# Another order of the Sync engine's transfers, and one small GpSimd sum moved, in a fused attention and feed-forward kernel

## The chip, the cores and the metric

The kernel runs on one core of one Trainium2 chip. The metric is the device time of one execution in microseconds (us). A core has five engines with an instruction stream each: TensorE (PE in the profile, with PEld for its weight loads), VectorE (DVE), ScalarE (ACT), GpSimd (POOL) and the Sync engine (SP), which computes nothing and here issues most of the DMA transfers. Engines meet only at semaphores.

## The reference, cut to what matters

There are 8 batches of 512 rows with 512 columns. `x` attends to the context `ctx` of its own batch, with a mask on the probabilities, and a quantised feed-forward layer follows; both add to `x`.

```python
n = _layernorm(x)                                   # rows of x, eps 1e-5
scores = einsum('bqd,bkd->bqk', n, ctx) / 0.72
attn = softmax(scores) * mask
o = einsum('bqk,bkd->bqd', attn, ctx) + attn_bias
x = x + einsum('bqd,de->bqe', o, weights)
n = _layernorm(x)
s = max(amax(abs(n), axis=-1), 1e-6) / 127.0
q = clip(round(n / s), -128, 127)                   # int8, one scale per row
x = x + (q @ weight_q.T) * s * weight_scale + ffn_bias
```

## The kernel before, in words

The 4096 rows are 32 tiles of 128 rows, four to a batch. A tile goes through the engines in one step each of several stages, so that in step `d` scores are made of tile `d`, its probabilities are used for attention a step or two later, the integers of tile `d-4` go through the feed-forward product, and the normalised rows of tile `d+1` and the context tile `d+4` are made ready. Products in float32 are made of three float32r products of a high and a low part (`product3`, lines 636 to 638), so each operand is split: ACT copies the high part (`ct_hi`, `xt_hi`, `pt_hi`, `vw_hi`), DVE or POOL subtracts it for the low part (`ct_lo`, `xt_lo`, `pt_lo`, `vw_lo`).

Every engine runs `step(base, d)` over the same tiles, written out by hand (`run_steps`): four steps of the head (tiles 0 to 3), three rounds of eight steps that form the loop (tiles 4 to 27), and the tail (tiles 28 to 31 and what is left). The order within a step is the order of the code; there is no scheduler.

Three operands have to be transposed. In the loop this is done by 32x32 blocks: a DMA brings blocks to the right place, 4 transfers of 64 KB, and a DVE transpose turns inside each block. The normalised rows take the way `x_norm` -> `norm_rows` in HBM (issued by ACT) -> `x_blocks` (SP, `load_rows`) -> DVE `xt_raw`. The probabilities take the way `probs` -> `prob_rows` in HBM (SP, `store_probs`) -> `p_blocks`, which is the memory of `wq_rows` in the rows of the profile (SP, `load_probs`) -> DVE `pt_raw` -> ACT `pt_hi` -> DVE `pt_lo` -> PE `ps_attn`. The context goes straight from its input to `ctx_in`, two tiles by 4 transfers of 128 KB, and DVE turns each tile into `ct_raw`. The integers `x1_int` (`x_int` in the profile) are turned by a DMA transpose (`turn_integers`).

So SP's step is a fixed list: on even `d` the context pair `d+4, d+5`; the integers of tile `d-4`, for which it waits for ACT line 970; the rows of `d+1`; the store of the probabilities of `d-1`; `x` of tile `d+4`; the mask of `d+2`; and the load of the probabilities of `d-1`, for which it waits until their store has landed (line 535). SP works one transfer at a time, so whatever stands behind a waiting one is late too. SP's step `d` runs while the other engines are in the later part of their step `d-1`: the probabilities it stores have just been made.

ACT's step ends with two DMA issues, and before the second it waits for POOL's `out_tile` (`add_up`, line 1526). POOL gets to `out_tile` only after `inverse_deviation` (lines 1569 and 1572, the 1/sqrt of the second layernorm), which waits for ACT's sum of squares (line 1017). ACT's next step begins with `ct_hi` (line 878), rounding (958) and the integers (970), and line 896 sums up the `x` tile `d+4` that SP has loaded.

In the tail the last tile (`LAST`, 31) goes in halves. Its scale on DVE (`gains`, line 1269) needs its rstd from POOL (line 1572).

Of the kernel before, what the change touches and what calls it, by code (L numbers as in the profile page):

```python
# [37 lines left out]
P = 128  # L38
# [3 lines left out]
BLOCK = 32  # L42
QUADS = P // BLOCK
# [53 lines left out]
def exists(base, n):  # L97

    return 0 <= base + n < TILES
# [17 lines left out]
def slot(n, ring):  # L117

    return (PHASE + n) % ring
# [68 lines left out]
def xattn_ffn_kernel(nc, x, ctx_rows, mask, weights, attn_bias, weight_q, weight_scale, ffn_bias, out):  # L188
# [8 lines left out]
    with ExitStack() as stack:  # L197
# [239 lines left out]
        def is_tile(base, n, tile):  # L437

            return isinstance(base, int) and base + n == tile
# [28 lines left out]
        def _(sp):  # L468
# [3 lines left out]
            def load_blocks(into, src, row, n, tiles, loaded):  # L472
# [4 lines left out]
                for b in range(QUADS):  # L477
                    blocks = into[b * BLOCK:(b + 1) * BLOCK, k:k + tiles, :]
                    sp.dma_start(blocks.rearrange("i t (a c) -> i (t a) c", a=QUADS),  # L479
                                 rows[:, :, b * P:(b + 1) * P]).then_inc(loaded[k // 2], 16)  # L480

            def load_rows(base, n, row):

                quads = norm_rows[bass.ds(row, P), :].rearrange("(a i) d -> i a d", i=BLOCK)
                wait_rows(sp, norm_rows_stored, base, n)
                for b in range(QUADS):
                    blocks = x_blocks[b * BLOCK:(b + 1) * BLOCK, slot(n, 4), :]
                    sp.dma_start(blocks.rearrange("i (a c) -> i a c", a=QUADS),  # L488
                                 quads[:, :, b * P:(b + 1) * P]).then_inc(x_blocks_loaded[slot(n, 2)], 16)
# [61 lines left out]
            def step(base, d, row):  # L551

                bounced = in_loop(base)
                n = d + 4
                if n % 2 == 0 and exists(base, n) and not is_tile(base, n, PER_BATCH) \
                        and not is_tile(base, n, PER_BATCH + 2):

                    wait_count(sp, ct_raw_ready, base, n - 4 + 2 - PER_BATCH)
                    load_blocks(ctx_in, ctx_flat, row + n * P, n, 2, ctx_loaded)
                n = d - 4  # L560
                if exists(base, n) and (in_loop(base) or base + n < BY_PE):
                    turn_integers(base, n)
                n = d + 1
                if is_tile(base, n, BY_PE_ROWS):

                    sp.wait_ge(w_lo_ready, NT)
                    sp.wait_ge(bias_terms_ready, NT)
                if exists(base, n) and not is_tile(base, n, 1) and (not last_batch(base) or d == 0):
                    load_rows(base, n, row + n * P)
                if bounced:  # L570
                    store_probs(base, d - 1, row + (d - 1) * P)
                n = d + 4
                if exists(base, n):

                    wait_count(sp, x1_ready, base, n - 8 + 1)
                    load_x(row + n * P, slot(n, 8))
                n = d + 2
                if exists(base, n):

                    wait_count(sp, probs_ready, base, n - 4 + 1)  # L580
                    load_mask(row + n * P, slot(n, 4))
                if is_tile(base, d, 1):
                    load_ffn_constants()
                    sp.wait_ge(wq_rows_ready, 1)
                    for o in range(NT):
                        sp.dma_start_transpose(wq_t[:, :, o * P:(o + 1) * P], wq_rows[:, o, :]) \
                            .then_inc(wq_turned, 16)
                if is_tile(base, d, PER_BATCH - 1):

                    sp.wait_ge(wq_turned, 16 * NT)  # L590
                if bounced:
                    load_probs(base, d - 1, row + (d - 1) * P)
                n = d - 5
                if is_tile(base, n + 1, LAST):
                    store_out(base, n, row + n * P)
                    for h in range(2):

                        sp.wait_ge(last_out_ready, h + 1)
                        sp.dma_start(out_rows[LAST * P:TILES * P, half_of(h)], last_out[:, half_of(h)]) \
                            .then_inc(last_stored, 16)  # L600
                elif last_batch(base) and d > 0:
                    store_out(base, n, row + n * P)
                if last_batch(base) and d < 2:
                    load_rows(base, d + 2, row + (d + 2) * P)
# [863 lines left out]
        def _(pool):  # L1468
# [51 lines left out]
            def step(base, d):  # L1520
# [109 lines left out]
                if last_batch(base) and exists(base, d - 1):  # L1630
                    if is_tile(base, d - 1, TAIL):
                        inverse_deviation(d - 2)
                    if not is_tile(base, d - 1, LAST):
                        inverse_deviation(d - 1)
                    if is_tile(base, d - 1, TAIL):
                        add_up(d - 4)
                        add_ffn_bias(d - 2)
                    else:
                        add_ffn_bias(d - 2)
                        add_up(d - 4)  # L1640
                    if is_tile(base, d - 1, LAST):
                        inverse_deviation(d - 1)
                    if is_tile(base, d - 1, LAST):
                        add_ffn_bias(d - 1)
                if is_tile(base, d - 2, LAST):
# [33 lines left out]
```

## Time and profile before

| | us |
|---|---|
| median of 3 runs | 329.21 (328.72 to 329.78) |
| the profiled execution, its time | 328.42 |
| the profiled execution, its span | 326.6 |
| PE busy | 311.9 (95%) |
| DVE busy | 261.0 (80%) |
| POOL busy | 259.3 (79%) |
| ACT busy | 240.6 (74%) |

The span runs from the first to the last instruction; 1.8 us of the execution lie around it. An engine's idle time matters only where somebody waits for that engine. In the timeline, a row is start, duration, engine, line, operation and tiles, and in brackets how long the engine sat idle before it and what ended that. "xN" after a row merges N of a kind. SPq and ACTq are the issue of DMAs by SP and ACT; a transfer lands later than its issue ends.

### The profile page before, as it was taken

Reading aid. Unit: us, or ns where it says so; the run is one execution under the profiler, and the core shown is the slowest. Engines: PE = TensorE matmul, PEld = TensorE weight load, DVE = VectorE, ACT = ScalarE, POOL = GpSimd, SP = SyncE. Lnnn points to the kernel's source line nnn. Section 1 sums busy time; section 2 is a strip of 40 time slices with the busy share of each in tenths; the row PEclk is TensorE's granted clock in tenths of the full one; section 3 lists DMA queues with packets and bytes.
Section 4 is the critical chain, followed back from the end, with each engine's and each line's share of the span. In section 5 each row is a group of like instructions: output and inputs, shape, how many; then the busy total and the mean of one; then the engine's idle time right before and its main releaser. Section 6 shows DMA issues by size and latency. Waiting matters only on the chain.

```text
span 326.6 us, 5339 instructions
## 1 busy us (share of the span) xinstructions
PE 311.9 (95%) x1418; PEld 239.5 (73%) x1418; DVE 261.0 (80%) x565; ACT 240.6 (74%) x494; POOL 259.3 (79%) x362
## 2 busy tenths in 40 slices
PE   8999989999999999899998999999999999999982
PEld 7888767777777678677776777767778676776671
DVE  2998765988886899688887888788888778879775
ACT  5467867887887788788876889788787878866440
POOL 3274587897999789799997989899898879858683
PEclk9999999999999999999999999999999999999999
DMA  7995985798968979997888969998897996451112
GB/s 215 264 228 186 200 216 192 220 219 249 247 202 261 238 228 194 271 229 232 259 243 228 265 200 238 243 251 237 244 243 201 234 241 192 147 159 49 50 63 98
DMA packets 88173, 68.39 MB, mean 209 GB/s; under 512 B 25040, under 2 KB 67792, under 8 KB 88144
## 3 DMA queue, kind: packets, MB, share of 16 engines
q1 hardware_dynamic: 80368, 53.90, 65.3%
q10 hardware_dynamic: 7776, 14.16, 12.0%
q8 instruction: 11, 0.18, 0.3%
q14 instruction: 18, 0.15, 0.2%
HBM read 41.16 MB, written 22.54 MB: 195 GB/s over the span
## 4 chain that ended last, share of the span: by engine, by line
SPq 24%; DMA 22%; POOL 15%; ACT 11%; issue 9%; PE 9%; DVE 7%; ACTq 1%; POOLq 0%; DVEq 0%
DMA prob_rows<-probs 10%; DMA wq_rows<-prob_rows 8%; SPq L488 8%; SPq L535 7%; POOL out_tile L1526 5%; SPq L543 5%; SPq L479 4%; ACT x_round L958 2%; ACT ps_ct L1017 2%; POOL rstd L1572 2%; DVE pt_raw L1223 2%; ACT ct_hi L878 2%; ACT x_int L970 2%; POOL x_in L1560 2%; DMA norm_rows<-x_norm 1%
## 5 line engine op out<-in xcount | busy, mean ns | idle before, releaser
L636 PE MATMUL ps_attn<-vw_hi,pt_hi 128*128 128x512 f32 x120 | 47.9, 399 | 3.6 <-DVE pt_lo L1123 3.6
L636 PE MATMUL ps_scores<-ct_hi,xt_hi 128*128 128x512 f32 x124 | 48.7, 393 | 1.1 <-POOL xt_lo L1541 1.0
L638 PE MATMUL ps_scores<-ct_hi,xt_lo 128*128 128x512 f32 x124 | 48.3, 389 | 0.0
L637 PE MATMUL ps_scores<-ct_lo,xt_hi 128*128 128x512 f32 x124 | 48.3, 389 | 0.0
L638 PE MATMUL ps_attn<-vw_hi,pt_lo 128*128 128x512 f32 x120 | 46.8, 390 | 0.0
L637 PE MATMUL ps_attn<-vw_lo,pt_hi 128*128 128x512 f32 x120 | 46.8, 390 | 0.0
L1248 DVE TENSOR_TENSOR probs<-ps_scores,mask_in 128x512 f32<-128x512 f32 x32 | 22.0, 687 | 26.7 <-ACT ps_scores L981 26.3
L878 ACT ACTIVATE ct_hi<-ct_raw 128x512 fp32r<-128x512 f32 x28 | 17.7, 632 | 33.1 <-POOL out_tile L1526 30.4
L1560 POOL TENSOR_TENSOR x_in<-x_in,bias_w 128x512 f32<-128x512 f32 x32 | 41.5, 1296 | 0.7 <-issue 0.7
L1541 POOL TENSOR_TENSOR xt_lo<-xt_raw,xt_hi 128x512 fp32r<-128x512 f32 x29 | 37.7, 1301 | 4.1 <-ACT xt_hi L913 4.1
L1526 POOL TENSOR_TENSOR out_tile<-ffn_out,x_plus 128x512 f32<-128x512 f32 x28 | 39.6, 1415 | 0.0
L1586 POOL TENSOR_TENSOR x_plus<-x,ffn_bias_wide 128x512 f32<-128x512 f32 x28 | 36.3, 1297 | 3.7
L1533 POOL TENSOR_TENSOR ct_lo<-ct_raw,ct_hi 128x512 fp32r<-128x512 f32 x28 | 36.7, 1309 | 2.8 <-ACT ct_hi L878 2.8
L1139 DVE STREAM_TRANSPOSE xt_raw<-x_blocks 128x512 f32<-128x512 f32 x30 | 33.1, 1103 | 1.1 <-DMA x_blocks<-norm_rows 1.1
L810 PE MATMUL ps_ffn<-wq_t,xq_t 128*128 128x512 bf16 x120 | 31.1, 382 | 0.8 <-ACT xq_t L952 0.7
L1139 DVE STREAM_TRANSPOSE ct_raw<-ctx_in 128x512 f32<-128x512 f32 x28 | 30.8, 1099 | 0.0
L636 PEld LDWEIGHTS ps_attn<-vw_hi,pt_hi 128*128 128x128 f32 x120 | 22.5, 188 | 11.0 <-DVE pt_lo L1123 6.5
L888 ACT ACTIVATE x_norm<-x_in,norm 128x512 f32<-128x512 f32 x32 | 25.7, 804 | 5.2 <-POOL norm L1508 5.2
L636 PEld LDWEIGHTS ps_scores<-ct_hi,xt_hi 128*128 128x128 f32 x124 | 23.3, 188 | 7.1 <-POOL xt_lo L1541 2.4
L958 ACT ACTIVATE x_round<-x_neg,round_magic,neg_gain 128x512 f32<-128x512 f32 x31 | 24.9, 803 | 3.7 <-DVE neg_gain L1277 3.7
L636 PE MATMUL ps_vw<-w_hi,ct_hi 128*128 128x512 f32 x64 | 27.3, 427 | 0.0
L638 PEld LDWEIGHTS ps_scores<-ct_hi,xt_lo 128*128 128x128 f32 x124 | 23.3, 188 | 4.9
(187 smaller groups left out, 820.8 us busy)
## 6 DMA issues: line engine op xcount, KB each, us to landing
x_in<-in_x_dram SPq DMA_DIRECT2D x32, 256.0 KB, 4.1
mask_in<-in_mask_BxSxS_fk_dram SPq DMA_DIRECT2D x32, 256.0 KB, 4.4
norm_rows<-x_norm ACTq DMA_DIRECT2D x30, 256.0 KB, 4.0
x_blocks<-norm_rows SPq DMA_DIRECT2D x120, 64.0 KB, 2.4
ctx_in<-in_ctx_dram SPq DMA_DIRECT2D x56, 128.0 KB, 3.9
prob_rows<-probs SPq DMA_DIRECT2D x24, 256.0 KB, 2.3
wq_rows<-prob_rows SPq DMA_DIRECT2D x96, 64.0 KB, 3.5
out_dram<-out_tile ACTq DMA_DIRECT2D x24, 256.0 KB, 4.3
```

Of the source, the lines that this page charges most:

```text
L488: sp.dma_start(blocks.rearrange("i (a c) -> i a c", a=QUADS), quads[:, :, b * P:(b + 1) * P]).then_inc(x_blocks_loaded[slot(n, 2)], 16)
L636: nc.tensor.matmul(bank_, lhs_hi(t), rhs_hi(t), start=(t == 0), stop=False)
L637: nc.tensor.matmul(bank_, lhs_hi(t), rhs_lo(t), start=False, stop=False)
L638: last = nc.tensor.matmul(bank_, lhs_lo(t), rhs_hi(t), start=False, stop=(t == NT - 1))
L810: last = nc.tensor.matmul(ffn_bank(base, n)[:, :], xq_t[:, slot(n, 2), t, :], wq_t[:, t, :], start=(t == 0), stop=(t == NT - 1))
L958: nc.scalar.activation(x1_round[:, slot(n, 2), :], x1_neg[:, slot(n, 2), :], ACT.Identity, bias=round_magic[:, 0:1], scale=col(neg_gain, n ...
L1139: nc.vector.transpose(into.rearrange("p t (a i) -> p t a i", a=QUADS), blocks.rearrange("p (a j t) -> p t a j", a=QUADS, t=NT)).then_inc(r ...
L1526: nc.gpsimd.tensor_tensor(out_tile[:, slot(n, 2), :], ffn_out[:, slot(n, 2), :], x1_plus_of(base, n), ALU.add).then_inc(out_ready, 1)
L1533: nc.gpsimd.tensor_tensor(ct_lo[:, batch_of(n), :, j * P:(j + 1) * P], ct_raw[:, slot(n, 2), :, :], ct_hi[:, batch_of(n), :, j * P:(j + 1) ...
L1541: nc.gpsimd.tensor_tensor(flat(xt_lo[:, slot(n, 2), :, :]), flat(xt_raw[:, slot(n, 2), :, :]), flat(xt_hi[:, slot(n, 2), :, :].bitcast(F32 ...
L1560: nc.gpsimd.tensor_tensor(x_in[:, slot(d, 8), :], x_in[:, slot(d, 8), :], bias_w[:, :], ALU.add).then_inc(x_plus_ready, 1)
L1586: nc.gpsimd.tensor_tensor(into, x1_of(base, n), ffn_bias_wide[:, :], ALU.add).then_inc(x1_plus_ready, 1)
```

## The change

SP's step is put in another order, in all steps of the loop. The store of the probabilities comes right behind the integers, ahead of the rows. Their load comes right behind the rows, ahead of `x` and the mask. The context pair is loaded at the end of the step, and its four transfers are parted: two at the end of an even step, two at the end of the odd one after it, and the pair that a step asks for is one further on (`n = d + 6 - d % 2`), so its first half is issued at the end of step `n-6` instead of all of it at the start of step `n-4`. The number of transfers, their sizes and their bytes stay.

The second part is on POOL in the tail: in the step behind the last tile's scores, `inverse_deviation` of the last tile stands ahead of the two sums `add_ffn_bias(d - 2)` and `add_up(d - 4)` instead of behind them.

```diff
+            def load_half_pair(base, n, h):
+                wait_count(sp, ct_raw_ready, base, n - 4 + 2 - PER_BATCH)
+                k = slot(n, 4)
+                rows = ctx_flat[bass.ds((base + n) * P, 2 * P), :].rearrange("(a i) d -> i a d", i=BLOCK)
+                for b in range(h * QUADS // 2, (h + 1) * QUADS // 2):
+                    blocks = ctx_in[b * BLOCK:(b + 1) * BLOCK, k:k + 2, :]
+                    sp.dma_start(blocks.rearrange("i t (a c) -> i (t a) c", a=QUADS),
+                                 rows[:, :, b * P:(b + 1) * P]).then_inc(ctx_loaded[k // 2], 16)
...
                 bounced = in_loop(base)
-                n = d + 4
-                if n % 2 == 0 and exists(base, n) and not is_tile(base, n, PER_BATCH) \
-                        and not is_tile(base, n, PER_BATCH + 2):
-
-                    wait_count(sp, ct_raw_ready, base, n - 4 + 2 - PER_BATCH)
-                    load_blocks(ctx_in, ctx_flat, row + n * P, n, 2, ctx_loaded)
                 n = d - 4
                 if exists(base, n) and (in_loop(base) or base + n < BY_PE):
                     turn_integers(base, n)
+                if bounced:
+                    store_probs(base, d - 1, row + (d - 1) * P)
                 n = d + 1
...
                     load_rows(base, n, row + n * P)
                 if bounced:
-                    store_probs(base, d - 1, row + (d - 1) * P)
+                    load_probs(base, d - 1, row + (d - 1) * P)
                 n = d + 4
...
-                if bounced:
-                    load_probs(base, d - 1, row + (d - 1) * P)
+
+                n = d + 6 - d % 2
+                if exists(base, n) and base + n >= 2 * PER_BATCH:
+                    load_half_pair(base, n, d % 2)
...
                     else:
+                        if is_tile(base, d - 1, LAST):
+                            inverse_deviation(d - 1)
                         add_ffn_bias(d - 2)
                         add_up(d - 4)
-                    if is_tile(base, d - 1, LAST):
-                        inverse_deviation(d - 1)
```

This is SP in the middle of the loop before: an even step with the context, then an odd one without. The line number is followed by the tile written and the tile read; `x4` are four transfers.

```order
L479 DMA ctx_in<-in_ctx_dram 32x8x128 x4
L543 DMA_TRANSPOSE xq_t<-x_int 128x4x128
L488 DMA x_blocks<-norm_rows 32x4x128 x4
L526 DMA prob_rows<-probs 128x512
L470 DMA x_in<-in_x_dram 128x512
L492 DMA mask_in<-in_mask_BxSxS_fk_dram 128x512
L535 DMA wq_rows<-prob_rows 32x4x128 x4
L543 DMA_TRANSPOSE xq_t<-x_int 128x4x128
```

The same engine in the same place now, one step and the first transfer of the next.

```order
L554 DMA_TRANSPOSE xq_t<-x_int 128x4x128
L537 DMA prob_rows<-probs 128x512
L499 DMA x_blocks<-norm_rows 32x4x128 x4
L546 DMA wq_rows<-prob_rows 32x4x128 x4
L470 DMA x_in<-in_x_dram 128x512
L503 DMA mask_in<-in_mask_BxSxS_fk_dram 128x512
L490 DMA ctx_in<-in_ctx_dram 32x8x128 x2
L554 DMA_TRANSPOSE xq_t<-x_int 128x4x128
```

The four context transfers of every second step have become two in every step, at its end. The store has moved ahead of four row transfers, and the load has moved ahead of `x` and the mask, so `x` now has four more transfers ahead of it.

The last instructions of POOL before; `out_tile` is the sum that is stored, `rstd` the 1/sqrt.

```order
L1526 TENSOR_TENSOR out_tile<-ffn_out,x_plus 128x512
L1586 TENSOR_TENSOR ctx_in<-x,ffn_bias_wide 128x512
L1526 TENSOR_TENSOR out_tile<-ffn_out,ctx_in 128x512
L1569 TENSOR_TENSOR var_eps<-meanvar,eps 128x1
L1572 TENSOR_TENSOR rstd<-var_eps,minus_half 128x1
L1586 TENSOR_TENSOR ct_raw<-ctx_in,ffn_bias_wide 128x512
L1526 TENSOR_TENSOR out_tile<-ffn_out,ctx_in 128x512 x2
```

And now:

```order
L1535 TENSOR_TENSOR out_tile<-ffn_out,x_plus 128x512
L1578 TENSOR_TENSOR var_eps<-meanvar,eps 128x1
L1581 TENSOR_TENSOR rstd<-var_eps,minus_half 128x1
L1595 TENSOR_TENSOR ctx_in<-x,ffn_bias_wide 128x512
L1535 TENSOR_TENSOR out_tile<-ffn_out,ctx_in 128x512
L1595 TENSOR_TENSOR ct_raw<-ctx_in,ffn_bias_wide 128x512
L1535 TENSOR_TENSOR out_tile<-ffn_out,ctx_in 128x512 x2
```

The two 1-column instructions have moved ahead of two 512-column ones.

## Rows read from the trace of the kernel before

**Rows 1.** Waits in the loop, 56 to 275 us: total, times, longest

```profile
PEld ps_attn L636 <- DVE pt_lo L1123: 6.5, 8, 1.4
...
DVE pt_raw L1223 <- DMA wq_rows<-prob_rows: 10.5, 11, 1.7
...
ACT ps_xt L896 <- DMA x_in<-in_x_dram: 1.1, 2, 0.6
```

**Rows 2.** Timeline of PE, the feed-forward product of three steps

```profile
57.33 1.04 PE L810 MATMUL ps_ffn<-wq_t,xq_t 128*128 128x512 bf16 x4
...
102.73 1.04 PE L810 MATMUL ps_ffn<-wq_t,xq_t 128*128 128x512 bf16 x4
...
273.35 0.82 PE L810 MATMUL ps_ffn<-wq_t,xq_t 128*128 128x512 bf16 x3
```

**Rows 3.** Windows, whole loop: busy by engine, PEclk, DMA share, GB/s

```profile
57.33:273.35 216.02, 212.40 (x921) 161.24 (x921) 179.41 (x391) 172.99 (x366) 188.56 (x253) 1.00 0.88 236
```

**Rows 4.** Timeline of SP, an odd step and the start of the even one

```profile
226.25 1.21 SPq L543 DMA_TRANSPOSE xq_t<-x_int  x1
227.50 1.99 SPq L488 DMA_DIRECT2D x_blocks<-norm_rows  x4
229.54 0.43 SPq L526 DMA_DIRECT2D prob_rows<-probs  x1
...
231.84 1.76 SPq L535 DMA_DIRECT2D wq_rows<-prob_rows  x4
233.65 2.65 SPq L479 DMA_DIRECT2D ctx_in<-in_ctx_dram  x4
236.40 1.19 SPq L543 DMA_TRANSPOSE xq_t<-x_int  x1
```

**Rows 5.** Timeline of ACT, then of DVE, in the same step

```profile
225.53 0.63 ACT L970 ACTIVATE x_int<-x_round 128x512 bf16<-128x512 f32 x1
...
227.26 0.59 ACT L896 ACTIVATE ps_xt<-x_in 128x512 f32<-128x512 f32 x1
...
235.00 0.63 ACT L970 ACTIVATE x_int<-x_round 128x512 bf16<-128x512 f32 x1
...
226.87 0.69 DVE L1248 TENSOR_TENSOR probs<-ps_scores,mask_in 128x512 f32<-128x512 f32 x1 [1.10 <-ACT ps_scores L981]
...
234.12 1.10 DVE L1139 STREAM_TRANSPOSE xt_raw<-x_blocks 128x512 f32<-128x512 f32 x1
...
237.86 0.70 DVE L1223 STREAM_TRANSPOSE pt_raw<-wq_rows 128x512 f32<-128x512 f32 x1
```

**Rows 6.** Timeline of ACT, the integers in two undisturbed steps

```profile
84.05 0.63 ACT L970 ACTIVATE x_int<-x_round 128x512 bf16<-128x512 f32 x1
...
92.99 0.63 ACT L970 ACTIVATE x_int<-x_round 128x512 bf16<-128x512 f32 x1
```

**Rows 7.** DMA issues of the page: count, KB each, us to landing

```profile
x_blocks<-norm_rows SPq DMA_DIRECT2D x120, 64.0 KB, 2.4
...
prob_rows<-probs SPq DMA_DIRECT2D x24, 256.0 KB, 2.3
wq_rows<-prob_rows SPq DMA_DIRECT2D x96, 64.0 KB, 3.5
```

**Rows 8.** Landings of the x_in transfers, 50 to 275 us

```profile
DMA to landing us min/median/max: 2.9/4.1/5.0
```

**Rows 9.** Timeline of POOL, DVE and SP at the end of the tail

```profile
317.15 0.55 POOL L1572 TENSOR_TENSOR rstd<-var_eps,minus_half 128x1 f32<-128x1 f32 x1
...
320.73 2.60 POOL L1526 TENSOR_TENSOR out_tile<-ffn_out,ctx_in 128x512 f32<-128x512 f32 x2 [1.81 <-DVE ffn_out L1202]
...
314.42 0.21 DVE L1304 BATCH_NORM_AGGREGATE meanvar<-last_stats 128x2 f32<-128x12 f32 x1
...
317.81 0.21 DVE L1269 TENSOR_SCALAR q_range<-abs_max,rstd 128x1 f32<-128x1 f32 x1 [1.70 <-POOL rstd L1572]
...
323.73 0.93 SPq L599 DMA_DIRECT2D out_dram<-ct_raw  x2
```

## The prediction, written before the changed kernel was run

> **What bounds the kernel now.** I read the waits of the loop first. PE's weight loads stop eight times for the low part of the probabilities, 6.5 us in all, and DVE stops eleven times, 10.5 us in all, for the transfer that brings the probabilities back from HBM [rows 1]. The reader is to see one name at both: the way of the probabilities is what comes late, and PE waits at its end. PE's own timeline gives the size. From 57.33 to 102.73 there are five steps, 9.08 us each; from 102.73 to 273.35 there are 18 in 170.62 us, 9.48 each [rows 2]. PE is busy for 212.40 of the 216.02 us [rows 3]. So 9.08 is PE's floor for a step, and the loop's 23 steps stand 216.02 - 23 x 9.08 = 7.2 us above it. That is all that an order of transfers can win there.
>
> Is there a second floor close by? ACT, POOL and DVE go round in a ring: sum of squares, rstd, `out_tile`, `ct_hi`, integers. In a stretch without waits for DMA the integers start at 84.05 and 92.99, 8.94 apart [rows 6]. That is only 0.14 below PE's 9.08, so what delays ACT by more than 0.14 in every step is seen in the time.
>
> Then SP's timeline says why the probabilities are late. Call S the start of the integers' transpose, 226.25; ACT made them at 226.16 (225.53 + 0.63), so SP is punctual [rows 4, 5]. It issues the rows until 229.49, the store until 229.97, `x` and the mask, waits for the store, loads the probabilities at 231.84 and, as the next step is even, the context at 233.65 for 2.65. It is through at 236.30, and the next transpose starts at 236.40, though its integers were there at 235.63: 0.8 late [rows 4, 5]. The last of the four loads is issued some 1.3 into its 1.76, at 233.2, and lands 3.5 later [rows 7], at 236.7; DVE wants it at 237.86 [rows 5]. A punctual step has 1.2 to spare, and one that starts 0.8 late, with some extra in a landing, has nothing.
>
> **The change in the loop, step by step from S.** The transpose is out at S + 1.25 (227.50). The store needs `probs`, ready at 226.87 + 0.69 = 227.56, S + 1.31 [rows 5]; SP notices some 0.1 later (226.16 against 226.25), so the store goes at S + 1.4. That is a new wait of 0.15, and everything in SP's step stands behind it. Rows: S + 1.87 to 3.86 (0.43 for the store, 1.99 for the four). The store lands 2.3 after its issue [rows 7], at S + 3.7, so the wait for it has gone behind the rows. Load: S + 3.9 to 5.66. `x`: at S + 5.7 for 0.43, and the mask about as long, to S + 6.6. Half the context: 2.65 / 2 = 1.3, to S + 8.0. The next integers come at S + 9.08, so SP has 1.1 to spare in every step, where before the pair of steps had no reserve in its even half.
>
> Who gets what, and when:
> The probabilities: last load at S + 5.2, landed at 8.7 with the same 3.5, wanted at 237.86 = S + 11.6. Spare 2.9 instead of 1.2. The waits of [rows 1] should go, and with them their echo on ACT, POOL and PE.
> The rows: last of four at S + 3.4, + 2.4 = S + 5.8, wanted at 234.12 = S + 7.9. Spare 2.1 instead of 2.7; no cost.
> The context: the second half is out at the end of a step and is wanted about a step and a half later; no cost, and the wait in front of it is for turns two steps old.
> `x` of tile d+4: this is the loser. It was issued at S + 3.8, right behind the store, and now goes at S + 5.7. ACT wants it at 227.26 + 9.08 = S + 10.1 [rows 5]. With the median landing of 4.1 it is there at S + 9.8, 0.3 early; with the longest, 5.0 [rows 8], 0.6 late. Before, ACT waited for it twice in the loop, 0.6 at most [rows 1], both times when SP was late. Bounds of this term: at 2.9 to 4.35 nothing; at 5.0, see the rivals. I take the median, as the store of 256 KB that stood right ahead of `x` is gone from there, and four loads of 64 KB stand there that SP needed 1.76 to issue.
>
> Here a rule of the Trainium skill speaks against the change: by "DMA: Bandwidth & Descriptors", section "Queues, rings and completion order", each DMA engine takes the descriptors of one issuer's queue in ring order, and goes round between the queues packet by packet. By that rule `x` now stands behind 256 KB more of its own queue in a step; had they not drained yet, at the loop's 236 GB/s they would add 1.1, and the sum would be that of rival B. The trace shows a store that lands in 2.3 right behind four row transfers of the same size, so such transfers have drained by the time they are issued.
>
> The first step of the loop: the store now waits there for probabilities that are made late in the head, and the rows behind it with it. ACT and DVE have time left against PE at that place, and I put it at 0, up to 0.5.
>
> I do not give the loop its floor. Landings scatter, and 0.14 of reserve on ACT's ring is little; I leave 0.03 per step, 0.7 in all. The loop: -7.2 + 0.7 = -6.5.
>
> **The change on POOL.** DVE waited 1.70 for the last tile's rstd, to 317.81 [rows 9]. The statistics that POOL needs are there at 314.42 + 0.21 = 314.63, and POOL's pair of small instructions takes under 1 us (the second ends at 317.70). Now it ends near 315.5, and DVE goes on with its next instruction 1.7 earlier. What is late next: POOL's last two sums, 2.60 long, start when DVE's product is there, but POOL's list ahead of them is as long as before and starts 0.2 later; and the output at 323.73 follows them. So not all of 1.7: I take 1.5, with 0 and 1.7 as ends. The two 512-column sums that move behind are wanted by nobody in the next 2 us but the stores.
>
> **The sum.** 328.42 - 6.5 - 1.5 = 320.4 for the profiled execution. The median of the runs is 0.8 above that execution, so in the runs' terms 321.2 (329.21 - 8.0).
>
> **Rivals.**
> A, the forecast: steps of 9.08 to 9.15. 321.2.
> B, `x` is late in most steps. For it: 0.3 of spare against a scatter of 1 in the landing, and the two waits of before. Against: it waited only in late steps. If it lands L after its issue, it comes at S + 5.7 + L and is wanted at S + 8.94 + 1.01 + the wait of the step before; so the mean wait is (5.7 + L - 9.95) / 2. At L = 5.0 that is 0.38, a step of 9.32, a loop of 214.4: -1.6, with the tail -3.1, 326.1.
> C, slower than before, by the same way but with stalls of SP's queue: the four context issues took 2.65 where four others took 1.99, and such stalls ahead of `x` add to L. It decides from a step of 9.46 on, where the loop has lost what the tail wins; that is a mean wait of 0.52, L and stall together 5.3. At 5.6 the step is 9.62, the loop 221.1, and the time 329.2 + 5.1 - 1.5 = 332.8.
> D, the order is not what matters: the 16 DMA engines have a share of 0.88 already [rows 3], and a faster step asks for 244 GB/s instead of 236; then the transfers stretch and the step stays at 9.39. Only the tail wins: 327.7. For it: the share. Against: the five steps at 9.08 carried the same bytes.
> On that the Trainium skill ("DMA: Bandwidth & Descriptors", section "Where 436 GB/s comes from") gives about 358 GB/s as HBM's limit for a core, far above both; by it D would fall away. No row here shows a rate near it, and I leave D its chance.
> E, the tail's gain is lost behind another wait while the loop does as forecast: 322.7. It lies within A's range.
>
> **Chances.** A 0.62 (with E), B 0.19, D 0.11, C 0.08. Least time: the loop at its floor, 1.7 in the tail, and half a microsecond of run-to-run luck: 319.3. So the range is 319.3 to 326.8; it leaves out C, D and a sliver. A difference of 0.3%, 1.0 us, is about what this measurement can tell from none. Faster by more than that: A, B and most of D, 0.87; the same: the rest of D and the border to C, 0.06; slower 0.07.
>
> **What would show it.** The gaps between PE's feed-forward products at 9.1 in all the loop; no wait of DVE for the probabilities' loads; SP waiting for ACT's integers in every step, not in every second one; the wait for the store next to nothing; ACT's waits for `x` few and under 0.3; the last q_range less than 0.1 behind its abs_max. I would be wrong if line 896 waits in most steps (B, C), if the four loads take over 2.5 to issue or land in over 6 (D), or if a wait turns up on the rows.

## The result: 340.71 instead of 329.5 us

The changed kernel takes 340.71 us (median of 4 runs, 338.01 to 343.77); the kernel before, in the same session on the chip, takes 329.5 (328.72 to 330.47). The ratio is 1.0311, with a 95% interval of 1.0237 to 1.0386: 3% slower, where 321.2 was forecast. Ratios and intervals count only the executions within 1.5% of their kernel's fastest, so here and below they are not the quotient of the two medians; the profiled execution of the changed kernel isn't one of them. The profiled execution took 343.77, with a span of 341.9, 15.3 above the span of before. It is 3.1 above its kernel's median, and the two medians are only 11.2 apart.

### The profile page after: what moved, and what is told of

The parts are those of the page before. It is cut to its first block, busy times and chain, and to the rows that moved or that the text cites. A ratio compares the mean times of both kernels' runs of the same rounds, so it can differ in the third digit from the quotient of the medians.

```text
span 341.9 us, 5324 instructions
## 1 busy us (share of the span) xinstructions
PE 316.2 (92%) x1403; PEld 239.1 (70%) x1418; DVE 263.4 (77%) x565; ACT 238.7 (70%) x494; POOL 264.0 (77%) x362
## 4 chain that ended last, share of the span: by engine, by line
DMA 31%; ACT 16%; POOL 14%; SPq 11%; issue 10%; PE 9%; DVE 6%; ACTq 1%; POOLq 0%; DVEq 0%
DMA x_in<-in_x_dram 15%; DMA prob_rows<-probs 14%; SPq L546 6%; POOL out_tile L1535 5%; POOL rstd L1581 3%; ACT x_round L967 3%; ACT ps_ct L1026 2%; ACT x_neg L1020 2%; DVE probs L1257 2%; ACT ps_scores L990 2%; ACT ct_hi L887 2%; ACT x_int L979 2%; ACT vw_hi L927 1%; SPq L554 1%; SPq L499 1%
## 5 line engine op out<-in xcount | busy, mean ns | idle before, releaser
L1535 POOL TENSOR_TENSOR out_tile<-ffn_out,x_plus 128x512 f32<-128x512 f32 x28 | 36.6, 1309 | 0.0
L905 ACT ACTIVATE ps_xt<-x_in 128x512 f32<-128x512 f32 x27 | 16.2, 599 | 23.2 <-DMA x_in<-in_x_dram 23.2
L819 PE MATMUL ps_ffn<-wq_t,xq_t 128*128 128x512 bf16 x105 | 27.7, 381 | 1.9 <-ACT xq_t L961 0.9
L645 PE MATMUL ps_ut<-w_hi,ct_hi 128*128 128x512 f32 x56 | 23.6, 421 | 4.7 <-POOL ct_lo L1542 3.8
```

Source lines behind the costliest of these rows:

```text
L645: nc.tensor.matmul(bank_, lhs_hi(t), rhs_hi(t), start=(t == 0), stop=False)
L819: last = nc.tensor.matmul(ffn_bank(base, n)[:, :], xq_t[:, slot(n, 2), t, :], wq_t[:, t, :], start=(t == 0), stop=(t == NT - 1))
L1535: nc.gpsimd.tensor_tensor(out_tile[:, slot(n, 2), :], ffn_out[:, slot(n, 2), :], x1_plus_of(base, n), ALU.add).then_inc(out_ready, 1)
```

## The profile of the changed kernel

Where the 15.3 are, by PE's feed-forward product. The lines are the first, the 22nd and the 24th of the loop, as in [rows 2].

```profile
58.66 0.81 PE L819 MATMUL ps_ffn<-wq_t,xq_t 128*128 128x512 bf16 x3
...
267.31 1.04 PE L819 MATMUL ps_ffn<-wq_t,xq_t 128*128 128x512 bf16 x4
...
287.62 1.04 PE L819 MATMUL ps_ffn<-wq_t,xq_t 128*128 128x512 bf16 x4
```

The first stands 1.3 later than before. Then 23 steps take 228.96, 9.95 each, where they took 216.02: 12.9 of the 15.3. Behind the loop 1.0 is lost. Part of it goes with a lower granted clock of TensorE in the last slice, 6 tenths where it was 9; the last tile's feed-forward product takes 1.28 there and took 1.03.

```profile
PEclk9999999999999999999999999999999999999996
```

So it is the loop, and nearly every step of it: they take 8.9 to 11.8, and three in four of them more than 9.4.

The waits of the loop, 56 to 275 us, all engines and then SP's queue (total, times, longest); they answer to [rows 1]:

```profile
ACT ps_xt L905 <- DMA x_in<-in_x_dram: 21.4, 19, 2.8
...
PEld ps_attn L645 <- DVE pt_lo L1132: 10.4, 11, 2.2
...
DVE pt_raw L1232 <- DMA wq_rows<-prob_rows: 0.9, 1, 0.9
```
```profile
SPq L546 <- DMA prob_rows<-probs: 33.7, 21, 2.6
SPq L552 <- ACT x_int L979: 11.1, 14, 1.4
```

The same wait of SP for its store, in the kernel before:

```profile
SPq L535 <- DMA prob_rows<-probs: 22.5, 23, 1.5
```

What was to go has gone: DVE waits 0.9 for the probabilities, not 10.5. Two others stand in its place. SP waits 21 times, 1.6 each, for its own store before it may load from HBM what it stored. It did so before too, 23 times and 1.0 each, but then `x` and the mask had gone out ahead of the wait; now `x`, the mask and the contexts stand behind it. ACT waits 19 times for `x`, 1.1 each, where it was 1.1 in the whole loop. The chain that ended last names the same two, 15% and 14% of the span:

```profile
DMA x_in<-in_x_dram 15%; DMA prob_rows<-probs 14%; SPq L546 6%; POOL out_tile L1535 5%; POOL rstd L1581 3%; ACT x_round L967 3%; ACT ps_ct L1026 2%; ACT x_neg L1020 2%; DVE probs L1257 2%; ACT ps_scores L990 2%; ACT ct_hi L887 2%; ACT x_int L979 2%; ACT vw_hi L927 1%; SPq L554 1%; SPq L499 1%
```

The page's landings (count, KB each, us from issue to landing), against [rows 7, 8]:

```profile
x_in<-in_x_dram SPq DMA_DIRECT2D x32, 256.0 KB, 4.7
...
prob_rows<-probs SPq DMA_DIRECT2D x24, 256.0 KB, 4.1
wq_rows<-prob_rows SPq DMA_DIRECT2D x96, 64.0 KB, 2.1
```

The store lands in 4.1 where the prediction had taken 2.3. One step of the timeline, SP, ACT and DVE, shows how it goes round:

```profile
206.80 0.63 ACT L979 ACTIVATE x_int<-x_round 128x512 bf16<-128x512 f32 x1
...
207.50 1.20 SPq L554 DMA_TRANSPOSE xq_t<-x_int  x1
...
208.13 0.69 DVE L1257 TENSOR_TENSOR probs<-ps_scores,mask_in 128x512 f32<-128x512 f32 x1 [1.61 <-ACT ps_scores L990]
...
208.85 0.47 SPq L537 DMA_DIRECT2D prob_rows<-probs  x1
208.96 0.60 ACT L905 ACTIVATE ps_xt<-x_in 128x512 f32<-128x512 f32 x1 [0.34 <-DMA x_in<-in_x_dram]
209.37 1.87 SPq L499 DMA_DIRECT2D x_blocks<-norm_rows  x4
...
212.58 1.73 SPq L546 DMA_DIRECT2D wq_rows<-prob_rows  x4
214.35 0.46 SPq L470 DMA_DIRECT2D x_in<-in_x_dram  x1
214.85 0.44 SPq L503 DMA_DIRECT2D mask_in<-in_mask_BxSxS_fk_dram  x1
215.34 1.02 SPq L490 DMA_DIRECT2D ctx_in<-in_ctx_dram  x2
216.24 0.63 ACT L979 ACTIVATE x_int<-x_round 128x512 bf16<-128x512 f32 x1
...
216.94 1.20 SPq L554 DMA_TRANSPOSE xq_t<-x_int  x1
...
218.29 0.47 SPq L537 DMA_DIRECT2D prob_rows<-probs  x1
218.80 0.60 ACT L905 ACTIVATE ps_xt<-x_in 128x512 f32<-128x512 f32 x1 [0.73 <-DMA x_in<-in_x_dram]
```

The rows are issued by 211.24, then SP stands for 1.3 until the store of 208.85 has landed. `x` goes at 214.35, 6.85 behind the start of the integers' transpose, the S of the prediction (S + 5.7 was forecast), and ACT stands for it until 218.80. ACT's sum of `x` is ahead, in its program, of everything that makes the integers of the next step, so a late `x` makes those late, then SP's transpose, and with it the next store, load and `x`. It is a ring over two steps: S to `x`, `x` to its sum, that sum to the S after the next.

The windows, the 21 steps to the 22nd product, against [rows 3]:

```profile
58.66:267.31 208.65, 196.39 (x829) 146.44 (x839) 164.60 (x357) 155.71 (x332) 175.46 (x230) 1.00 0.92 221
```

The DMA engines are busy for a higher share, 0.92 against 0.88, at a lower rate, 221 against 236 GB/s. The clock is 1.00; PE is simply idle more.

And the tail, against [rows 9]: POOL's two small instructions and sums, and DVE's work on the last tile.

```profile
329.46 0.21 DVE L1313 BATCH_NORM_AGGREGATE meanvar<-last_stats 128x2 f32<-128x12 f32 x1
...
330.02 0.55 POOL L1581 TENSOR_TENSOR rstd<-var_eps,minus_half 128x1 f32<-128x1 f32 x1
...
331.18 0.21 DVE L1278 TENSOR_SCALAR q_range<-abs_max,rstd 128x1 f32<-128x1 f32 x1
...
331.77 1.27 POOL L1535 TENSOR_TENSOR out_tile<-ffn_out,ctx_in 128x512 f32<-128x512 f32 x1
331.88 1.31 DVE L1321 TENSOR_SCALAR x_round<-x_neg,neg_gain 128x256 f32<-128x256 f32 x1
333.00 1.31 POOL L1595 TENSOR_TENSOR ct_raw<-ctx_in,ffn_bias_wide 128x512 f32<-128x512 f32 x1
333.22 1.24 DVE L1327 TENSOR_SCALAR x_int<-x_round 128x256 bf16<-128x256 f32 x1
334.38 0.34 DVE L1321 TENSOR_SCALAR x_round<-x_neg,neg_gain 128x256 f32<-128x256 f32 x1
...
334.75 0.29 DVE L1327 TENSOR_SCALAR x_int<-x_round 128x256 bf16<-128x256 f32 x1
```

The last `q_range` has no wait now, 1.7 sooner against `meanvar`. But the first halves of `x_round` and `x_int` take 1.31 and 1.24, and the second halves, the same work, 0.34 and 0.29. Each long one ends 0.15 behind the sum of POOL that was under way (333.04, 334.31). From `meanvar` to the end of the last `x_int` it is 5.58; before, it was 5.57. Of the 1.7 nothing is left. The kernel before had the same thing once, smaller:

```profile
317.67 1.26 POOL L1586 TENSOR_TENSOR ct_raw<-ctx_in,ffn_bias_wide 128x512 f32<-128x512 f32 x1
...
318.50 0.57 DVE L1312 TENSOR_SCALAR x_round<-x_neg,neg_gain 128x256 f32<-128x256 f32 x1
```

This first half took 0.57 and ended 0.14 behind POOL's sum.

## The experiments

Two theories stood for the loop. **Q**, queue order: the load behind its own store makes SP wait, and puts that wait ahead of `x`. **W**: the 16 DMA engines are at their limit, and an even spread of the transfers hurts. In the first expectation Q is told differently: there it begins with a store that lands late behind reads from HBM, and "everything else follows". The results below take that half away, and what is left is the Q of this paragraph. The first four kernels ran beside a kernel before of 328.16.

**One part alone: the context halves.** Only they go to the end of the step, a step sooner.

```
-  (start of even steps) load_blocks(ctx_in, ..., 2 tiles)
+  (end of each step)    load_half_pair(base, d + 6 - d % 2, d % 2)
```

> Only the context in halves at the end of each step, one step sooner; everything else in the order of before. Theory Q (the store of the probabilities lands late when reads of HBM for x, mask and context were put into SP's queue right ahead of it; everything else follows): here the rows' 2 us still stand between the context and the store, so the store lands in 2.3 to 2.8 us, x is issued right behind it, and SP is punctual in every step: steps of 9.1 to 9.25 us, 322 to 326 us. Rival W (the 16 DMA engines are at their limit, and an even spread of the context lets every landing stretch): landings of x and store grow as in the changed kernel, steps of 9.7 or more, 335 us or more.

Measured: 326.93, ratio 0.9957 (0.9901 to 1.0013). No harm by itself, and at most a small gain, where Q gave 322 to 326. SP still waits 23.2 for its store, in 23 steps, as before; the store lands in 2.3, and W, which gave 335 or more, is out for this order.

**One part alone: the store ahead of the rows.**

```
                turn_integers(base, n)
+               store_probs(base, d - 1, row + (d - 1) * P)
                ...load_rows(...)
-               store_probs(base, d - 1, row + (d - 1) * P)
```

> Only the store of the probabilities ahead of the rows; the load stays at the end and the context at the start of even steps. Q: in even steps the store goes out 1.25 us behind four context transfers and lands in 4 us or more, in odd steps in about 2.5; the load behind x and mask hardly waits for it in odd steps and up to 1 us in even ones; x is issued as early as before, so the time is near before, 326 to 331 us. W: nothing changes in what is asked of the engines, 329 us. A rival R (the rows behind the store come late and DVE waits for them): 333 us or more with waits of DVE for x_blocks.

Measured: 321.22, ratio 0.9847 (0.9816 to 0.9878). The steps of PE are 9.08 almost throughout, and the wait for the store is 1.7 in all. This one edit gives what was forecast for the whole change. I had expected 326 to 331, nearly 5 too slow at the least. The store did land later where I said so, though in less than 4: mostly in 3.1 to 3.4 in the steps in which it is issued 1.3 to 2.1 behind four context transfers, and mostly in 2.2 to 2.4 in the others. But the load asks for it only 3.6 behind its issue, and so a landing of 3.4 costs nothing.

**One part alone: the load ahead of `x` and the mask.**

```
                ...load_rows(...), store_probs(...)
+               load_probs(base, d - 1, row + (d - 1) * P)
                ...load_x(...), load_mask(...)
-               load_probs(base, d - 1, row + (d - 1) * P)
```

> Only the load of the probabilities ahead of x and mask; the store stays behind the rows, so the load waits the store's whole 2.3 us at once. Q: x goes out at 7.6 us after the step's start instead of 3.8; with a landing of 4.1 ACT waits for it by 0.9 us a step in the mean, steps of 9.7 to 9.9 us, 336 to 341 us, although the store itself lands in 2.3 us. W: 329 us, as no transfer was added or spread.

Measured: 355.31, ratio 1.0808 (1.0688 to 1.0929). The waits in the loop, of SP and of ACT:

```profile
SPq L535 <- DMA prob_rows<-probs: 51.4, 20, 4.0
```
```profile
ACT ps_xt L896 <- DMA x_in<-in_x_dram: 30.8, 19, 2.9
```

With the store still right ahead of the load, SP stands for all of its landing, 2.6 a step. SP waited for ACT's integers once only, 0.8: here SP itself is the bound, at 10.5 a step. I had expected 336 to 341, by ACT's wait for `x` alone; that SP's own list no longer fits into the step I had not seen. The page's landing of the store is 2.9, so the loss does not need a store that lands late. The harmful edit is this one.

**The change without it.** Store, rows, `x`, mask, load, context halves, and POOL's edit.

```
-               load_probs(...)          (behind load_rows)
                ...load_x(...), load_mask(...)
+               load_probs(...)
```

> The changed kernel with the load of the probabilities behind x and mask again (order: integers, store, rows, x, mask, load, half a context pair). Q: x is issued at 3.9 us of the step and no longer waits for the store, and the load waits for the store only to some 5.5 us; steps of 9.1 to 9.3 us, 321 to 326 us, even if the store takes 3 to 4 us. W: as the changed kernel, 335 us or more.

Measured: 320.11, ratio 0.9815 (0.9781 to 0.9848). Q gave 321 to 326 and W 335 or more, so W falls. Here the loop's transfers go as evenly as in the changed kernel and faster, and the DMA share is 0.88 at 240 GB/s. The store lands in 2.7, though two context transfers stand right ahead of it.

The next four ran beside a kernel before of 328.38. **`x` alone moved**, ahead of the load; mask and contexts stay right ahead of the next store. The rival S says that a late landing of the store stalls SP and what comes behind, whatever that is:

```
                ...load_rows(...)
-               load_probs(...)
                ...load_x(...)
+               load_probs(...)
                ...load_mask(...), load_half_pair(...)
```

> The changed kernel with one transfer in another place: x ahead of the load of the probabilities; the mask and the context halves stay behind that load and right ahead of the next store. Theory Q (x decides, because behind the load it waits for the store's landing first): x is issued at 3.9 behind the integers and is there 4 later, the load waits 1.5 to 2 for the store as before, SP's work of 7.4 a step with that wait still fits into 9.08, and the time is 320 to 323. The rival S (the store lands late because mask and context halves are in the queue right ahead of it, and its late landing stalls SP and what comes behind): the landing stays 4 and more, the mask and the contexts are late instead of x, and the time is 330 or more.

Measured: 321.33, ratio 0.9779 (0.9739 to 0.9819). SP's waits and the landing of the store:

```profile
SPq L546 <- DMA prob_rows<-probs: 12.6, 20, 1.4
```
```profile
prob_rows<-probs SPq DMA_DIRECT2D x24, 256.0 KB, 3.6
```

SP still waits in 20 steps for a store that lands late (3.6), and it costs nothing, since `x` is ahead of the wait and ACT never waits for it. One transfer of 256 KB, put ahead of the load, is worth 19 us by the medians of the two sessions, 17 to 18 by their ratios. Theory Q holds, S does not.

**The change without its context edit.** The pair of tiles goes at the start of the even steps again; all else as changed.

> The changed kernel with the context tiles where they were (a pair of tiles ahead of the integers in every second step); store ahead of the rows, load ahead of x and mask, GpSimd's edit stay. Theory Q: x stays behind the load and so behind the store's landing, so the time stays far above before, 335 to 350; in every second step the integers and the store go 2 later, behind four context transfers. The rival, that the context halves at the step's end are what makes the changed kernel slow (five loads in a burst right ahead of the store): back to 328 or less.

Measured: 334.84, ratio 1.0200 (1.0151 to 1.0248), just at the low end of what Q gave. The rival, back to 328 or less, is out. The changed kernel's ratio, from another session, is 1% higher, and the two intervals just touch; so it is likely but not shown that the context halves, harmless alone, cost it that much. The store lands in 3.4 here and in 4.1 there.

**Why the store lands late.** The context halves are moved into the time in which SP waited for the store, away from the next store. A kernel before of 328.04 ran beside it.

```
                ...load_rows(...)
+               load_half_pair(...)
                load_probs(...), load_x(...), load_mask(...)
-               load_half_pair(...)
```

> The changed kernel with the context half loads moved from the step's end to between the rows and the load of the probabilities: SP issues them, 1.0 a step, in the time in which it waited for the store (1.6 a step), and they no longer stand right ahead of the next store. The step follows from a ring over two steps, integers to x, x to its sum, sum to the next integers but one: 7.36 + 4.76 + 8.09 = 20.2, 10.1 a step in the changed kernel. Theory L (the store's landing of 4.1 is the backlog of the reads right ahead of it): the landing falls to 3.0 or so, the load goes out at 4.6 to 5.0 in place of 5.4, and so x at 6.7; 19.4 for the ring, 9.7 a step, 333 to 336. The rival T (the landing comes from the traffic of the whole step, wherever it stands): the landing stays at 4 or more, the contexts behind the store delay it and the load too, and the time stays at 340 or more.

Measured: 337.81, ratio 1.0299 (1.0235 to 1.0362); the span of the profile is 335.4. Its landing and SP's waits:

```profile
prob_rows<-probs SPq DMA_DIRECT2D x24, 256.0 KB, 2.5
```
```profile
SPq L552 <- ACT x_int L978: 42.0, 21, 3.3
SPq L546 <- DMA prob_rows<-probs: 0.4, 2, 0.3
```

Theory L, that the reads right ahead of the store make it late, holds for the landing against T, the traffic of the whole step: the same bytes in a step, and the store lands in 2.5, not 4.1. But more moved than the contexts. SP now waits 2.0 a step for ACT's integers, and so the last read is issued 3.2 ahead of the store in the mean, where it was 2.0 in the changed kernel. The run does not tell whether the fewer bytes or the longer time does it. The time of this kernel is a little above my 333 to 336. SP's wait of 1.6 is gone, but 1.0 of issuing stands there instead, so `x` goes only 0.55 sooner. By its intervals this kernel isn't told apart from the changed one. Its steps are 9.74 against 9.95, but the 9.95 are of an execution 3.1 above its kernel's median, so they don't tell them apart either.

**The store ahead of the integers too.** The edit is made in the changed kernel and, below, in the fastest one (319.24, told of further down), beside a kernel before of 328.31.

```
+               store_probs(...)
                turn_integers(base, n)
-               store_probs(...)
```

> The changed kernel with the store of the probabilities one place further up, ahead of the integers: it is issued 1.3 or more sooner, the load behind it waits so much less of its 1.6 a step, and x goes out so much sooner although it stays behind the load and the mask and the context halves stay at the step's end. Theory Q (x is late by what the load waits for the store): the 1.1 a step that ScalarE waits for x go nearly, the step falls from 9.94 to 9.1 to 9.4, and the time to 321 to 329. The rival (the four large reads issued in one burst right ahead of the next step make x late by themselves, whatever the load waits): x_in keeps a landing of 4.7 or more and the time stays over 334.

Measured: 342.32, ratio 1.0411 (1.0353 to 1.0469): a miss. Waits of SP in the loop:

```profile
SPq L537 <- DVE probs L1257: 37.4, 20, 3.5
SPq L546 <- DMA prob_rows<-probs: 0.9, 3, 0.3
```

The wait for the landing went, as I wanted, and one for the probabilities themselves, 1.9 a step, came in its place, now with integers, rows and `x` behind it. I had not looked at when the probabilities are ready, though the prediction has it, at S + 1.31: in the step shown above they are done at 208.82, 1.3 behind the start of the integers' transpose. The marks of the rival came too, an `x` that lands in 4.6 and a time over 334; but with `x` at S + 5.56 that landing costs nothing by the prediction's formula (9.07 a step, worked out below), so the loss is the wait for the probabilities.

> z2_psum with the same edit, the store ahead of the integers. In z2_psum every step takes TensorE's 9.08 and the store is waited for 0.9 in all, so by theory Q nothing is left to gain: 319.2 within 0.3%. A gain beyond that, or a loss, would say that the store's place still decides something there.

Measured: 331.48, ratio 1.0105 (1.0046 to 1.0164), where 319.2 was expected: a miss for the same reason. SP waits 35.4 for the probabilities, the load is late at its end, and DVE waits 13.9 for it, as in [rows 1]. A full floor hid that the place of the store had no slack on the other side.

**The tail: POOL's edit alone.**

```
+                       if is_tile(base, d - 1, LAST): inverse_deviation(d - 1)
                        add_ffn_bias(d - 2); add_up(d - 4)
-                   if is_tile(base, d - 1, LAST): inverse_deviation(d - 1)
```

> The kernel before with GpSimd's edit alone (rstd of the last tile ahead of the two sums of the tiles before it). The port theory: q_range starts 1.4 to 1.7 sooner, but x_round and x_int of the first half then run beside GpSimd's out_tile and ct_raw sums, are held until each of these ends, and take 1.1 to 1.4 each in place of 0.57 and 0.29; the last x_int ends at the same distance from meanvar (5.6), the time is that of before, ratio 1.000. The prediction's tail: the wait of 1.70 goes and nothing comes in its place, 1.5 less, ratio 0.9955, and 4.1 from meanvar to the last x_int.

Measured: 329.56 against 328.38, ratio 1.0003 (0.9965 to 1.0041), as the port theory had it. Its tail, DVE and POOL:

```profile
317.29 1.31 DVE L1312 TENSOR_SCALAR x_round<-x_neg,neg_gain 128x256 f32<-128x256 f32 x1
318.63 1.24 DVE L1318 TENSOR_SCALAR x_int<-x_round 128x256 bf16<-128x256 f32 x1
...
317.18 1.26 POOL L1526 TENSOR_TENSOR out_tile<-ffn_out,ctx_in 128x512 f32<-128x512 f32 x1
318.41 1.30 POOL L1586 TENSOR_TENSOR ct_raw<-ctx_in,ffn_bias_wide 128x512 f32<-128x512 f32 x1
```

The same two long halves beside the same two sums, and again 5.58 from `meanvar` to the last `x_int`. No gain of this edit is to be seen in the trace or in the time.

**The tail with the port freed.** The kernel without the harmful edit (320.11), with the rounded value of the last tile in a free PSUM bank:

```
-  tensor_scalar(x1_round[half], x1_neg[half], ...); tensor_scalar(x1_int[half], x1_round[half], ...)
+  tensor_scalar(ps_vw[half],    x1_neg[half], ...); tensor_scalar(x1_int[half], ps_vw[half],    ...)
```

> The kernel x4_xmask (the change with the load of probabilities behind x and the mask) with the rounded value of the last tile written to a free PSUM bank and read from there, so that neither of VectorE's two operations has both sides in SBUF. The port theory: x_round and x_int take 0.3 to 0.6 per half although GpSimd's sums run beside them, 4.0 to 4.3 from meanvar to the last x_int in place of 5.6, and the time is 1.3 to 1.5 below the 320.1 of x4_xmask: 318.7. The rival, that something else than a shared port holds them (GpSimd takes SBUF bandwidth from any VectorE operation, or the first half waits for something that ends by chance with GpSimd's sums): they take 1.2 to 1.3 as in the changed kernel, and the time stays 320.1.

Measured: 319.24, ratio 0.9723 (0.9684 to 0.9761), the fastest kernel of this study. Its tail:

```profile
305.78 0.21 DVE L1313 BATCH_NORM_AGGREGATE meanvar<-last_stats 128x2 f32<-128x12 f32 x1
...
308.09 1.27 POOL L1535 TENSOR_TENSOR out_tile<-ffn_out,ctx_in 128x512 f32<-128x512 f32 x1
308.20 0.49 DVE L1321 TENSOR_SCALAR ps_vw<-x_neg,neg_gain 128x256 f32<-128x256 f32 x1
308.72 0.42 DVE L1327 TENSOR_SCALAR x_int<-ps_vw 128x256 bf16<-128x256 f32 x1
...
309.57 0.42 DVE L1327 TENSOR_SCALAR x_int<-ps_vw 128x256 bf16<-128x256 f32 x1
```

POOL's sums run beside them as before, and the halves take 0.49 and 0.42. From `meanvar` to the last `x_int` it is 4.21 in place of 5.58. So the trace has 1.4 of the 1.5 that the prediction gave to this part, by another edit on top of POOL's. The two times, 320.11 and 319.24, are from different sessions and differ by 0.9; the PSUM edit was not run side by side with the kernel that it is put on.

## Why the prediction was wrong

**The ring, in numbers.** Means over the loop's steps, taken from SP's and ACT's timelines, so halves of the three columns' sum differ from the measured step by up to 0.16; the prediction's formula for the mean wait, (S to `x` + landing - 9.95) / 2, with the second column as the landing, added to the ring of 8.94, stands beside the measured step.

| kernel | S to `x` | `x` to its sum | sum to the S after the next | formula | step |
|---|---|---|---|---|---|
| forecast | 5.7 | 4.1 | 7.93 (2 x 8.94 - 9.95) | below PE's 9.08 | 9.11 |
| changed | 7.36 | 4.76 | 8.09 | 10.03 | 9.95 |
| contexts early | 6.81 | 4.74 | 7.96 | 9.74 | 9.74 |
| contexts in pairs | 6.67 | 4.63 | 8.10 | 9.62 | 9.62 |
| store ahead of integers | 5.56 | 4.65 | 9.85 | 9.07 | 9.96 |
| `x` ahead of the load | 4.10 | 5.83 | 8.31 | below PE's 9.08 | 9.07 |
| load behind `x` and mask | 4.08 | 5.94 | 8.30 | below PE's 9.08 | 9.10 |

In the first four measured rows ACT waits for `x` in most steps (19, 17, 12 and 18 times in the profiles), and where it waits the second column is the landing and a little more; in the last two `x` is early and lies there. The formula gives the step within 0.1 in three of the four. That is less of a test than it looks, since with these columns it says only that the third stays near 7.93. It does, at 7.96 to 8.10, while the first goes from 6.67 to 7.36: this is the ring. In the fourth row the third column grew by 1.8, SP's wait for the probabilities. So the working of rival B was right, and its inputs were not. With the median landing of 3.7 from the page in place of 4.63, the row of contexts in pairs would come to 9.15, not 9.62: a mean formula with a median landing misses much where ACT waits in half of the steps.

1. "The store lands 2.3 after its issue [rows 7], at S + 3.7, so the wait for it has gone behind the rows." This step failed. The 2.3 of [rows 7] was measured behind four row transfers of 64 KB, with the mask or the contexts 3 and more ahead of it. Moved ahead of the rows, the store stands, in the step shown, 1.9 to 4 behind the context halves, the mask and `x`, 768 KB of reads, and lands in 4.1. SP waits 1.6 a step, and `x` goes at S + 7.36, not 5.7. The place of the load ahead of `x` turned this wait into a loss: with `x` ahead, a landing of 3.6 cost nothing.

2. I set aside the Trainium skill's rule of ring order ("DMA: Bandwidth & Descriptors", section "Queues, rings and completion order") with "such transfers have drained by the time they are issued". The trace showed that for row transfers of 64 KB and not for reads of 256 KB. The experiment with the contexts moved agrees with the rule: 2.5 against 4.1 with the same bytes in a step. And I weighed the rule only for `x`, where it would have cost 1.1, and not for the store, for which SP waits. Even for `x` the sum was not that of rival B: a landing of 4.1 + 1.1 = 5.2 gives a step of 9.42 by the formula, some 328 in all, outside my range.

3. `x`, "with the median landing of 4.1". It was 4.76 to ACT's sum, 4.7 as the page's median. Load, `x`, mask and contexts now go out as one burst behind the wait; that this makes `x` land later is not shown, and with the contexts ahead of the load it was still 4.74. With S + 5.7 and this landing the formula still gives 9.2 a step, rival B; both errors together give 10.0, beyond rival C, which stopped at 9.62 since it had no wait in it.

4. "The waits of [rows 1] should go": right for DVE, 10.5 to 0.9. PE's went up, 6.5 to 10.4; DVE now has the probabilities in time, so the likely cause is ACT, late by its waits for `x`.

5. Rival D, the DMA share: wrong. At 240 GB/s and a share of 0.88 the steps are 9.08.

6. PE's floor of 9.08, and 7.2 us above it as all that an order can win in the loop: right, and nearly all of it won by the store alone (321.22). The least time has a slip: floor, 1.7 and half a microsecond off 329.21 make 319.8, not 319.3.

7. The tail: "what is late next" named POOL's list and the output, and took 1.5. It was DVE itself. This is what the Trainium skill says in "SBUF — State Buffer", section "SBUF: two separate sides": VectorE, in a mode that uses two ports or with two inputs in SBUF, and GpSimd share a pair of ports as an exclusive lock, held for a whole instruction by the one that starts first. The trace agrees, with 1.31 and 1.24 for halves that take 0.34 and 0.29 alone, and the run through PSUM bears it out. The trace does not name the mode that DVE was in. My edit had brought DVE's instructions beside two POOL sums, and I had asked only who waits for the sums. The half of 0.57 in the kernel before was there to be read.

The chances were off as well: 0.07 for slower was too little for an edit that puts a wait for DMA into the queue that issues everything else.

What stays open: how the landing follows from what is ahead in the queue. It was 2.5, 2.7, 3.4, 3.6 and 4.1 in five orders of the same transfers (3.0 in another kernel with the order of the 2.7), and it tends to be longer with more reads ahead and a shorter time since the last: 2.5 where `x` and mask were issued last, 3.2 ahead of the store in the mean, and 3.6 where mask and contexts were, 2.0 ahead.

## What to carry to other kernels

A load that must wait for a store is best put at the end of an issuing queue, behind everything that doesn't need it: here, with the store early and the load late, SP waited 0.4 us for it in the whole loop, and with the load early each transfer behind it paid the rest of the landing. The store, in turn, can't go ahead of what makes its data. A landing read from a trace holds for what stood ahead of the transfer then; when the transfer is moved behind large reads, leave room for more: here 2.3 became up to 4.1. And when a POOL instruction is moved, ask which DVE instructions it now runs beside, not only who waits for it.

## What was new of the hardware

- A store of 256 KB landed in 2.5 to 4.1 us (medians), by its place among the other transfers of its queue, at equal bytes per step.
- A DVE `tensor_scalar` of 128x256 with both sides in SBUF that started just behind a POOL sum was held to 0.15 us behind the end of that sum: 0.34 became 1.31, 0.29 became 1.24. With one side in PSUM it took 0.49 or 0.42 with POOL at work.
- The DMA share was no measure of what the engines carried: from 57 to 275 us it was 0.92 at 222 GB/s in the changed kernel, 0.96 at 241 with `x` ahead of the load, and 0.88 at 240 with the load behind `x` and mask.
